# A graph network and expert layers on one core: preparing x for layer 0, and counting edge heads, rearranged

## The reference, cut to what matters

```python
x = x + gnn(_layernorm(x), weights, roots, biases, ln_gamma, ln_beta, [src, dst], edge_type)   # x: (3125, 256) f32
x = x + ffn(_layernorm(x))                      # 8 experts, top 2, 256 -> 512 -> 256

# gnn: 4 layers, 4 relations, 100000 edges sorted by dst; cnt = edges per (dst, relation)
inv_deg = 1.0 / max(cnt[dst, etype], 1)
for l in range(4):
    h = einsum('ni,rio->rno', X, W[l]);  msg = h[etype, src] * inv_deg
    out = segment_sum(msg, dst) + X @ root[l] + bias[l]
    X = elu(layernorm(out) * gamma[l] + beta[l]) + X
```

## Time and profile before

| | |
|---|---|
| three executions, median | 2614.72 us (2608.05 to 2615.36) |
| span of the profiled execution | 2581.8 us |
| TensorE busy | 2075.7 us, 80% |
| VectorE busy | 1572.2 us, 61% |
| GpSimd busy | 1253.4 us, 49% |
| ScalarE busy | 818.3 us, 32% |
| flag made, in the profiled execution | 65.4 us |

### The profile page before, as it was taken

The page is one execution under the profiler, slowest core; times in us unless marked ns, Lnnn a source line. Parts: engine busy times, 40 slices in busy tenths (PEclk is TensorE's granted clock), DMA queues, the critical chain, the costliest instruction groups (busy, mean ns, idle before and its releaser), DMA issues. The chain is left out here.

```text
span 2581.8 us, 46238 instructions
## 1 busy us (share of the span) xinstructions
PE 2075.7 (80%) x16327; PEld 1296.1 (50%) x16327; DVE 1572.2 (61%) x4475; ACT 818.3 (32%) x1674; POOL 1253.4 (49%) x1223
## 2 busy tenths in 40 slices
PE   0576788787879889898889888898987988774992
PEld 0334455454545455555545545454554645454992
DVE  5976677575656356566553656566364766575665
ACT  1564556454456011111111212111011111123992
POOL 2124333544430266666716666662665656752441
PEclk9988899988889899899989999999997999986996
DMA  5698333444432487666637867765775655532335
GB/s 144 187 273 256 115 112 115 133 123 125 122 112 98 145 256 233 219 210 210 187 113 249 257 210 240 236 218 158 230 231 165 181 163 169 179 101 64 95 94 178
DMA packets 211755, 445.56 MB, mean 173 GB/s; under 512 B 40819, under 2 KB 137088, under 8 KB 209733
## 3 DMA queue, kind: packets, MB, share of 16 engines
q1 hardware_dynamic: 138357, 274.65, 34.6%
q0 software_dynamic: 61408, 156.79, 20.1%
q10 hardware_dynamic: 11760, 11.08, 1.7%
HBM read 338.14 MB, written 103.90 MB: 171 GB/s over the span
## 5 line engine op out<-in xcount | busy, mean ns | idle before, releaser
L1421 POOL DMA_INDIRECT n_BIG<-n_xd,n_SIDX x1080 | 1110.9, 1029 | 1091.2 <-PE n_PS L1907 501.3
L1888 PE MATMUL n_PS<-n_BIG 125*128 125x500 f16 x4800 | 1196.8, 388 | 69.3 <-issue 45.3
L1888 PEld LDWEIGHTS n_PS<-n_BIG 125*128 125x128 f16 x4800 | 441.1, 100 | 508.7 <-issue 142.0
L1907 PEld LDWEIGHTS n_PS<-n_OW,n_BIG 128*128 128x128 f16 x4320 | 256.3, 99 | 204.6 <-issue 68.9
L1907 PE MATMUL n_PS<-n_OW,n_BIG 128*128 128x84 f16 (+21 forms) x4320 | 303.5, 201 | 51.5 <-issue 41.6
L1927 PE MATMUL n_PS<-n_BIG,n_tabs 128*128 128x256 f16 x2400 | 299.3, 280 | 19.4 <-issue 18.9
L1601 DVE TENSOR_TENSOR n_ST<-n_PS,n_INVB 128x500 f32<-128x500 f32 x200 | 199.9, 1041 | 158.4 <-issue 47.6
L1927 PEld LDWEIGHTS n_PS<-n_BIG,n_tabs 128*128 128x128 f16 x2400 | 239.7, 101 | 62.9 <-issue 29.0
L1627 DVE SCALAR_TENSOR_TENSOR n_U<-n_PS,n_cw,n_BI 125x256 f32<-125x256 f32 x100 | 48.2, 482 | 334.9 <-PE n_PS L1927 161.3
L1296 ACT ACTIVATE n_BIG<-n_PS 128x500 f16<-128x500 f32 x300 | 164.3, 578 | 195.5 <-PE n_PS L1859 93.6
L1312 ACT ACTIVATE n_tabs<-n_ST 128x1000 f16<-128x1000 f32 x100 | 103.8, 1038 | 358.8 <-DVE n_ST L1601 192.3
(11 more groups left out here) (271 smaller groups left out, 2252.9 us busy)
## 6 DMA issues: line engine op xcount, KB each, us to landing
n_BIG<-n_a SPq DMA_DIRECT2D x175, 625.0 KB
n_a<-n_BIG SPq DMA_DIRECT2D x12, 3125.0 KB
n_xg<-n_tabs SPq DMA_DIRECT2D x53, 481.9 KB
n_INVB<-n_ind SPq DMA_DIRECT2D x100, 250.0 KB
n_BIG<-n_xd,n_SIDX POOLq DMA_INDIRECT x1080
n_BIG<-in_L_ffn_W_dram SPq DMA_DIRECT2D x32, 512.0 KB
n_xd<-n_BIG SPq DMA_DIRECT2D x75, 112.0 KB
n_whl<-n_BIG SPq DMA_DIRECT2D x16, 512.0 KB
```

What stands on the lines that cost most here:

```text
L1421: e.indirect_dma_start(m.GR[:, g % GS, :], None, m.XD[l % 2][:, :], bass.IndirectOffsetOnAxis(ap=m.SIDX[:, i:i + 1], axis=0)).then_inc(s[f ...
L1888: ins = e.matmul(m.bank(2 * p + h, 0, W), m.xps[l % 2][0:TN, part, D * k + 128 * h:D * k + 128 * h + 128], m.RA[0:TN, c.slot_of(n), W * (k ...
L1907: ins = e.matmul(m.bank(2 * p + h, at, c.width[q]), m.GR[:, g % GS, D * part + 128 * h:D * part + 128 * h + 128], ow, start=(first == 0 an ...
```

## The change

The heads no longer go through DRAM. VectorE multiplies the heads, laid out over (125 columns k, 25 heads), with the diagonal of the identity, so that partition p holds its 25 heads in columns of k = p and zeros elsewhere; TensorE multiplies a matrix of ones with that in seven f32 calls of up to 512 columns, which puts all 3125 heads on all 128 partitions in PSUM. The counting reads PSUM. VectorE no longer normalizes x: it makes the factor and the offset of each row, and ScalarE normalizes (Identity with scale and bias, 25 instructions) as soon as these are there; the reciprocal roots and these offsets are made ahead of `scales_near`. The high and low halves of x for layer 0, and their store, move into the order, in fifths of five tiles, amid the build of tile 0. With 197 slots the places are: high halves (ScalarE) after slots 16, 32, 49, 65 and 82; low halves (VectorE) and the store (SyncE) after 78, 98, 118, 137 and 157. In the dense program, which isn't taken with these inputs, some register loads are changed.

```diff
@@ Near.steps, pick
                         if s == first_built // 2:
                             later(time["pe"], "far", 0, 0)
+                        for k in range(5):
+                            if s == first_built * (1 + k) // 12:
+                                order.append(("high0", 0, k))
+                                run("act", 1.5)
+                            if s == first_built * (4 + k) // 10:
+                                order.append(("low0", 0, k))
+                                order.append(("xstore0", 0, k))
+                                run("dve", 1.6)
@@ prep_sync
-    e.wait_ge(s["heads"], 1)
-    for p, n in ROWS:
-        e.dma_start(m.HD.rearrange("(p e) -> p e", p=TN)[p:n], m.HDS[p:n, :]).then_inc(s["hd"], 16)
-    e.wait_ge(s["hd"], 32)
-    e.dma_start(m.HB, m.HD.partition_broadcast(128)).then_inc(s["hd"], 16)
@@ prep_scalar
-    e.wait_ge(s["scales"], 1)
+    e.wait_ge(s["norm"], 1)
     for t in range(T):
-        e.wait_ge(s["ln"], t + 1)
-        e.activation(m.halves(0, t)[0], m.X[0:TN, t, :], ACT.Copy, scale=m.scale[0:TN, 0:1]).then_inc(s["hi0"], 1)
+        e.activation(m.X[0:TN, t, :], m.X[0:TN, t, :], ACT.Identity, bias=m.nt[0:TN, 0, t:t + 1],
+                     scale=m.nt[0:TN, 3, t:t + 1]).then_inc(s["ln"], 1)
@@ prep_tensor
+    e.wait_ge(s["heads"], 1)
+    for at in range(0, NH, 512):
+        n = min(512, NH - at)
+        ins = e.matmul(m.PS[:, at:at + n], m.ONF, m.HM[:, at:at + n], start=True, stop=True)
+    ins.then_inc(s["hd"], 1)
@@ prep_vector
-    e.tensor_copy(m.HDS[:, :], m.DST[:, 0:NE // TN:HEAD]).then_inc(s["heads"], 1)
+    q.did(e.tensor_copy(m.HDS[:, :], m.DST[:, 0:NE // TN:HEAD]))
+    q.did(e.memset(m.ONF, 1.0))
+    e.tensor_tensor(m.HM..., m.HDS.unsqueeze(1)..., m.ident[0:TN, 0:TN].unsqueeze(2)..., ALU.mult).then_inc(s["heads"], 1)
...
-        q.did(e.tensor_scalar(m.CMP[:, 0:high - low], m.HB[:, low:high], ...
+        q.did(e.tensor_scalar(m.CMP[:, 0:high - low], m.PS[:, low:high], ...
...
+    rsqrt(e, q, m, m.mv0[0:TN, :, 1], m.nt[0:TN, 3, :])
+    e.scalar_tensor_tensor(m.nt[0:TN, 0, :], m.mv0[0:TN, :, 0], -1.0, m.nt[0:TN, 3, :], ALU.mult, ALU.mult
+                           ).then_inc(s["norm"], 1)
     scales_near(e, q, m, s)
-    rsqrt(e, q, m, m.mv0[0:TN, :, 1], m.nt[0:TN, 3, :])
...
-    for t in range(T):
-        e.tensor_scalar(m.X[0:TN, t, :], m.X[0:TN, t, :], m.mv0[0:TN, t, 0:1], m.nt[0:TN, 3, t:t + 1],
-                        ALU.subtract, ALU.mult).then_inc(s["ln"], 1)
@@ sync_program
-    for part in range(2):
-        e.wait_ge(s["xp"], T)
-        for p, n in ROWS:
-            e.dma_start(m.XD[0][...], m.xps[0][p:n, part, :]...).then_inc(s["xd0"], 16)
+        elif what == "xstore0":
+            e.wait_ge(s["xp"], i + 1)
+            for part in range(2):
+                rows = m.XD[0][5 * TN * i:5 * TN * i + 5 * TN, D * part:D * part + D].rearrange(...)
+                for p, n in ROWS:
+                    e.dma_start(rows[p:n], m.xps[0][p:n, part, 5 * D * i:5 * D * i + 5 * D]...).then_inc(s["xd0"], 16)
@@ scalar_program
+    e.wait_ge(s["scales"], 1)
+    e.wait_ge(s["ln"], T)
     for what, l, i in c.order:
+        if what == "high0":
+            e.activation(m.fifth(0, i)[0], m.X[0:TN, 5 * i:5 * i + 5, :], ACT.Copy, scale=m.scale[0:TN, 0:1]
+                         ).then_inc(s["hi0"], 1)
@@ gpsimd_program
-                e.wait_ge(s[f"xd{l % 2}"], (64, 32 * T, 64 + 32 * T, 64 * T)[l])
+                e.wait_ge(s[f"xd{l % 2}"], (320, 32 * T, 320 + 32 * T, 64 * T)[l])
@@ vector_program
-    for t in range(T):
-        hi, lo = m.halves(0, t)
-        e.wait_ge(s["hi0"], t + 1)
-        e.scalar_tensor_tensor(lo, m.X[0:TN, t, :], m.scale[0:TN, 0:1], hi, ...).then_inc(s["xp"], 1)
+        elif what == "low0":
+            hi, lo = m.fifth(0, i)
+            e.wait_ge(s["hi0"], i + 1)
+            e.scalar_tensor_tensor(lo, m.X[0:TN, 5 * i:5 * i + 5, :], m.scale[0:TN, 0:1], hi, ...).then_inc(s["xp"], 1)
@@ tensor_program
-    e.wait_ge(s["ln"], T)
```

More of the change, by code:

```diff
@@ L57 @@
 PADE = 4096
-PREP = """dst src ety heads hd keys ev table off rows_near rows_far rel bad flag_pe flag x_in consts scales ln
+PREP = """dst src ety heads hd keys ev table off rows_near rows_far rel bad flag_pe flag x_in consts scales norm ln
 hi0 xp xd0 pool_const v_own b1 fc""".split()
@@ L685, in __init__ @@
         self.EV = dram("ev", (2 * (NE + PADE),), F32)
-        self.HD = dram("hd", (NH,), F32)
         self.IND = dram("ind", (T, W), F32)
@@ L844, in two, with fifth @@
         return at.rearrange("p (j d) -> p j d", j=2)
+    def fifth(self, l, k):
+        return [self.xps[l % 2][0:TN, a, 5 * D * k:5 * D * k + 5 * D] for a in range(2)]
     def halves(self, l, t):
@@ L971, in prep_vector @@
     e.wait_ge(s["dst"], 32)
-    e.tensor_copy(m.HDS[:, :], m.DST[:, 0:NE // TN:HEAD]).then_inc(s["heads"], 1)
+    q.did(e.tensor_copy(m.HDS[:, :], m.DST[:, 0:NE // TN:HEAD]))
+    q.did(e.memset(m.ONF, 1.0))
+    q.then()
+    e.wait_ge(s["pool_const"], N_CONST)
+    e.tensor_tensor(m.HM.rearrange("p (k e) -> p k e", k=TN), m.HDS.unsqueeze(1).broadcast_to([TN, TN, NH // TN]),
+                    m.ident[0:TN, 0:TN].unsqueeze(2).broadcast_to([TN, TN, NH // TN]), ALU.mult
+                    ).then_inc(s["heads"], 1)
     e.wait_ge(s["src"], 32)
@@ L983, in prep_vector @@
     e.scalar_tensor_tensor(m.EVS[:, :, 0], m.DST, 100.0, m.KF, ALU.mult, ALU.add).then_inc(s["keys"], 1)
-    e.wait_ge(s["hd"], 48)
+    e.wait_ge(s["hd"], 1)
     e.wait_ge(s["table"], 16)
     for i, (low, high) in enumerate(c.heads):
-        q.did(e.tensor_scalar(m.CMP[:, 0:high - low], m.HB[:, low:high], m.tb[:, 0, i:i + 1], 0.0, ALU.is_lt, ALU.add,
+        q.did(e.tensor_scalar(m.CMP[:, 0:high - low], m.PS[:, low:high], m.tb[:, 0, i:i + 1], 0.0, ALU.is_lt, ALU.add,
                               accum_out=m.cn[:, 0, i:i + 1]))
@@ L1002, in prep_vector @@
         q.did(e.bn_aggr(m.mv0[0:TN, t, :], m.bs0[0:TN, t, :]))
-    scales_near(e, q, m, s)
+    q.then()
     rsqrt(e, q, m, m.mv0[0:TN, :, 1], m.nt[0:TN, 3, :])
     q.then()
+    e.scalar_tensor_tensor(m.nt[0:TN, 0, :], m.mv0[0:TN, :, 0], -1.0, m.nt[0:TN, 3, :], ALU.mult, ALU.mult
+                           ).then_inc(s["norm"], 1)
+    scales_near(e, q, m, s)
     e.wait_ge(s["rows_near"], 16 * c.PT)
@@ L1066, in scales_near @@
     e.sem_inc(s["scales"], 1)
-PREP_DONE = dict(dst=32, src=32, ety=32, heads=1, hd=48, keys=3, ev=48, table=16, off=1, rel=1, bad=1, x_in=32,
-                 consts=32, b1=16, fc=32, scales=1, ln=T, hi0=T, pool_const=N_CONST)
+PREP_DONE = dict(dst=32, src=32, ety=32, heads=1, hd=1, keys=3, ev=48, table=16, off=1, rel=1, bad=1, x_in=32,
+                 consts=32, b1=16, fc=32, scales=1, norm=1, ln=T, pool_const=N_CONST)
 def prep_over(e, c, s):
@@ L1147, in sync_program @@
             e.dma_start(m.AD[i], m.RA[:, at:at + 5, :].rearrange("p a b -> p (a b)")).then_inc(s[f"store{i % 2}"], 16)
+        elif what == "xstore0":
+            e.wait_ge(s["xp"], i + 1)
+            for part in range(2):
+                rows = m.XD[0][5 * TN * i:5 * TN * i + 5 * TN, D * part:D * part + D].rearrange("(t p) d -> p t d", p=TN)
+                for p, n in ROWS:
+                    e.dma_start(rows[p:n], m.xps[0][p:n, part, 5 * D * i:5 * D * i + 5 * D].rearrange(
+                        "p (t d) -> p t d", d=D)).then_inc(s["xd0"], 16)
         elif what == "ind":
@@ L1766, in tensor_program @@
             e.wait_ge(s["sev"], i + 1)
-            e.wait_ge(s["lo"], c.place[l - 1, t] + 1) if l else e.wait_ge(s["xp"], t + 1)
+            e.wait_ge(s["lo"], c.place[l - 1, t] + 1) if l else e.wait_ge(s["xp"], t // 5 + 1)
             turned = m.bank(2 * c.pair_of[i], 0, 256).bitcast(F16)
@@ L1884, in dense_step @@
     if i == 0:
-        e.wait_ge(s["lo"], c.place[l - 1, k] + 1) if l else e.wait_ge(s["xp"], k + 1)
+        e.wait_ge(s["lo"], c.place[l - 1, k] + 1) if l else e.wait_ge(s["xp"], k // 5 + 1)
     for h in range(2):
@@ L2657, in dense_scalar @@
     e.wait_ge(s["prep"], c.prep["gp_sub"])
-    regs = [e.alloc_register(f"er{TD}_{i}") for i in range(BATCH)]
     for t in range(TD):
@@ L3092, in dense_tensor @@
     e.wait_ge(s["prep"], c.prep["b1t"])
-    regs = [e.alloc_register(f"pr{TD}_{i}") for i in range(3 * BATCH)]
+    regs = [e.alloc_register(f"pr{TD}_{i}") for i in range(2 * BATCH)]
     n_os = 0
@@ L3096, in dense_tensor @@
         n = min(BATCH, c.P - p0)
-        for w in range(3):
+        for w in range(2):
             at = w * c.PT * 128 + p0
@@ L3107, in dense_tensor @@
                 e.wait_ge(s["os"], n_os) if n_os else None
-                last = 2 * BATCH + min(i + 1, n - 1)
-                e.wait_ge(s["evac"], e.snap(regs[last], min_val=1, max_val=c.G + 1))
+                last = 2 * c.PT * 128 + p0 + min(i + 1, n - 1)
+                e.wait_ge(s["evac"], e.value_load(m.tabrow[0:1, last:last + 1], min_val=1, max_val=c.G + 1))
```

17 lines of the change are left out of this document (7 added, 10 removed).

## The result

Six executions of the changed kernel took 2582.06 to 2602.27 us, median **2585.46 us**; six of the kernel before, beside them, 2608.05 to 2619.20, median 2614.31. The same pair in three later groups of runs gave 0.9891, 0.9931 and 0.9929. The ratios are those on record, taken over all executions of a group; they aren't quotients of medians (here 0.9890, 28.9 us), so a time worked out from a ratio and one taken between medians can differ by some us. One execution of a later kernel (`spread_before`), 4536.87 us where the other five took 2266 to 2277, is left out of its ratio.

A forecast was written before the change was run, and what follows sets the result against it. The chain to the flag, then VectorE, full in tile 0's build, were taken as the bound. Terms -22.9 + 7.2 + 1.5 + 1.0 = -13.2 us gave 2601.5 us from 2614.72, range 2591 to 2617.

The forecast's parts named there:

- The order: Layer 0 after tile 0: jobs swap places by a few slots; no readable sign, 5 us either way.
- Rival C: Layer 0: new order puts a far tile's finish ahead of its inverse, each wait 10.1 us; 2626.7 us, chance 0.13.
- D: More gain: fast f32 (-2.4), high halves fully covered (-1.5), good order (-3); gain 20, 2594.6 us, chance 0.08.
- Heads: Preparation: product 3.6 us, TensorE 8, heads in PSUM at 19.1 us; f32 rate could make it 2.4 worse or 2.8 better.
- PSUM reads at 1.4 times: Counting: PSUM reads might take 1.4 times per element, 3 us in all; no difference taken, 3 us the far end.
- Loads and gathers: Preparation: x lands by 22 to 24 us, so statistics aren't held; GpSimd's gathers start at 26 to 28.
- 1.6 us of cover: Before the flag: far rows gathered by 42.7 us at the latest and needed at 44.3.
- Normalizing: On ScalarE: 10.08 us for 25 instructions plus 1.3 table load, ending 50.3, 3.2 after the flag; 1.9 us of gain lost.
- -22.9: Start of tile 0's build: VectorE begins at 54.0 instead of 76.88 us, a gain of 22.9 us.
- The build: Tile 0's build: low halves add 7.2 us, high halves 1.5 (0 to 6.2); some 74.5 + 9 us long.
- The store and the queue: SyncE's nearly full queue in tile 0's build: +1.0 us, bounds 0 and 6; tile 0's counts waited for under 8.
- Rival A: SyncE's zero-fill queue, not VectorE, sets when the first inverses land: gain 6, time 2608.7 us, chance 0.17.

The follow-up runs named there:

- spread_before: The kernel before with its 54 zero fills at every fourth block instead of each of the first 54; 0.9883 of the kernel before.
- no_cost: The changed kernel without the planner's two added costs, so the order of before but for the fifths; 0.9956 of the kernel before.
- same_near: The kernel before with only the changed dense program, which isn't taken; 1.0003 of the kernel before.
- spread_after: The changed kernel with its 54 zero fills at every fourth block instead of each of the first 54; 0.9794 of the kernel before.
- no_cost_2: The changed kernel without the planner's two added costs, run again on chip three; 0.9941 of the kernel before.
- after_3: The changed kernel itself, run again on chip four as reference; 0.9929 of the kernel before.
- spread_after_2: The changed kernel with zero fills at every fourth block, run again on chip four; 0.9764 of the kernel before.

## Why the prediction was wrong

The sign and the mechanism of the front were right; the time was 2585.46 against 2601.5, and the range missed it. By how much it missed is partly chance: the ratio of 0.9909 makes 2590.5 us of 2614.31, its interval reaches to 2597.6, and the 0.9931 and 0.9929 of later groups would give 2596, inside the range. Step by step:

**The order: the step that failed.** The prediction put it that "jobs after tile 0 swap places by a few slots. It has no sign that I can read", with 5 us either way. The sum took it at nothing. Measured by itself, it is -13.9 us (0.9946) and -10.2 us (0.9961), each clear of no change, and again 0.53% with thin fills. On top of the front it is 0.65% once and 0.10% once, so its size in the changed kernel is known only roughly, and by what waits it gains stays open. 3375 jobs move, some inverses by about 200 places. Seven or eight microseconds on a planner's clock are small; what they do to a list built by comparing due times isn't. A wider bound could have been taken from the earlier trace rows, where one wait behind a finish is 10.1 us. Rival C had this very place with the other sign; only D allowed the good one, 3 us.

**Heads.** The product took 3.42 us for 3.6, TensorE 8.34 for 8, and the first count starts at 18.92 for 19.1. The end at stake, PSUM reads at 1.4 times, isn't there: 447 elements take 0.68 us from PSUM as from SBUF. The pitch of the weight loads of L947 halves on the way:

```profile
14.96 0.34 PEld L947 LDWEIGHTS n_PS<-n_BIG 125*128 125x128 f32 x1 [0.52 <-issue]
15.82 0.34 PEld L947 LDWEIGHTS n_PS<-n_BIG 125*128 125x128 f32 x1 [0.52 <-issue]
16.41 0.19 PEld L947 LDWEIGHTS n_PS<-n_BIG 125*128 125x128 f32 x1 [0.26 <-issue]
16.84 0.19 PEld L947 LDWEIGHTS n_PS<-n_BIG 125*128 125x128 f32 x1 [0.24 <-issue]
```

0.86 us for an instruction of 512 columns, then 0.43. By the Trainium skill, "FP8 and Floating Point Precision", section "TensorE Precision Notes", an f32 product takes four passes; an estimate from it, with two passes taken for each of the two instructions of a call, is 0.85 us at 1.2 GHz and 0.43 at 2.4. The trace agrees, at the lower rate first and the higher after, and the whole, 8.34 us, lies between the prediction's 10.4 and 5.2. TensorE had been idle until 10.54 and was busy without a gap from there. The windows view gives a granted clock of 1.00 for both stretches, but the first clock that this trace records is 1.00 from 16.1 us on: the 1.00 ahead of it is no reading. The same holds for the 1.00 of the earlier trace rows; the first record of that trace is at 116.3 us.

**Loads and gathers.** x was there: the statistics waited 0.30 us, at 26.23 for 26.0. `EV` came later than forecast, at 30.40 for 26 to 28. The "1.6 us of cover" of the far rows (its own terms, 28 + 11.5 + 3, give 1.8) was therefore used up, and VectorE waited 1.10 us for them at 45.54. With the flag at 48.4 for 47.1, this is that miss nearly whole.

**Normalizing.** Two errors that cancel in part: the table load ran at 15.84, beside other work, and costs nothing, but Identity, with a scale and a bias for each partition and f32 out, takes 12.40 us for 25, not 10.08; which of these it is, no run separates. It ended at 51.7 for 50.3. The first one-hot came at 53.5 for 54.0 all the same, since ScalarE's first copy followed at once, where 1.1 us was allowed, and the four copies took 1.81 us for 2.5. For the term of -22.9 the traces show -23.4 (76.88 to 53.53).

**The build.** Low halves 1.57 us each for 1.45, high halves 1.35 for 1.25; the prediction's own slopes give 1.51 and 1.31. From the first one-hot to the last pair it took 77.2 us against 71.9 in the trace of before (148.8 less 76.9): 5.3 us longer for 8.7 (the prediction's 74.5 reaches 2.6 us past the last pair). VectorE was busy 69.49 us of the build before and 75.37 after:

```profile
53.50:130.70 77.20, 45.47 (x218) 24.75 (x219) 75.37 (x260) 53.67 (x120) 0.00 (x0) 0.65 0.68 170
```

The granted clock of this stretch is 0.65, and TensorE is busy 45.47 us of the 77.20: it isn't what bounds the build.

**The store and the queue: mis-sized.** +1.0 was taken, 0 to 6 bounded. The counts' wait grew by 8.3 us (5.6 to 13.9), and 8.6 in `no_cost` against `same_near`. The text said "the counts of tile 0 may come later" and named their bound as under 8; the profile after breaks it, and `spread_after` shows the zero fills as the cause. The gathers, the other fear, were free: the twelve were issued by 147.6 and the next waited for a chunk, at 157.52. The last fifth's four issues, eight fills and one small load keep SyncE from 120.19 to 137.60, and the counts, issued at 137.64, release TensorE at 149.3 only.

So the front's own sum was right by its two ends: -13.2 forecast, -11.4 (`no_cost`, 0.9956) and -15.4 (`no_cost_2`, 0.9941) measured. That is luck in part: the build's term was 3 us too long and the store's 7 us too short. By the first chunk the changed kernel is 10.3 us ahead (157.0 for 167.3); what the ends show above that these runs don't explain. Rival A, that the zero fills give the gain back, was true in part: about 8 of 23 us go that way, and thin fills give back more than that. What the sum lacked was one term, the order's, with bounds that weren't taken from any row.

## What to carry to other kernels

Where a list is written by a planner, a change to its costs is an edit of its own: write the list out before and after, look where the jobs behind the longest waits have gone, and give the term at least those waits as a bound, in both directions. What is taken from the front and put into a full stretch is worth what the next shared queue leaves of it: read when the small, urgent transfer is issued, not only how busy the engines are. And a span and a median of other executions aren't two readings of one thing; ask how far a span is from its own execution's time.

## What the hardware showed unexpectedly

The same kernel, the one before, takes 2614, 2580, 2295, 2614 and 2300 us in the five groups of runs, 14% from end to end. On the quick chips TensorE's busy time is 1986.7 us against 2099.1 for the changed kernel, and its clock 0.937 against 0.911 (`after_3` and the profile after). TensorE's idle time that the profile puts down to "issue" is nearly absent there: 0.7 us from 130 to 740 us in `spread_after_2`, against 26.0 for the pair steps alone in `no_cost_2`. The rest of the difference these runs don't explain.

A loaded queue holds up its issuer: behind the 3125 KB store of tile 0's matrix four fills of 482 KB take SyncE 16.90 us to issue after, where in the thinned version the one behind the same store takes 1.41 us and the others up to there 0.4 to 0.6, and the 24 KB of counts, issued behind six fills, release TensorE 11.6 us after their issue.

```profile
131.29 0.87 SPq L1158 DMA_DIRECT2D n_tabs<-n_BIG  x1
132.69 1.41 SPq L1232 DMA_DIRECT2D n_xg<-n_tabs  x1
```

These two rows are SyncE's in `spread_after_2`: the counts go out 6.3 us sooner than after, and TensorE's wait for them isn't among its longest.
